# Expert weights split during the first attention, its stack laid out in one piece, and one batch instead of two held for the end

## What is computed

```python
x = x + attn0(layernorm(x))        # 16 heads, weights replaced by their signs times a mean
x = x + cross0(layernorm(x), ctx)
x = x + ffn0(layernorm(x))
x = x + attn1(layernorm(x))        # 4 global and 12 windowed heads
x = x + cross1(layernorm(x), ctx)
x = x + moe(layernorm(x))
...
shared = jax.nn.silu(xt @ sg_w.T) * (xt @ su_w.T) @ sd_w.T
logits = xt @ router_w.T + routing_bias
topk_p, topk_idx = jax.lax.top_k(jax.nn.sigmoid(logits), 2)     # of 8 experts
h = jax.nn.silu(einsum('th,eih->tei', xt, wg)) * einsum('th,eih->tei', xt, wu)
routed = einsum('te,teh->th', w, einsum('tei,ehi->teh', h, wd))  # w: the two normalised probabilities
return shared + routed
```

## Time and profile before

| | |
|---|---|
| median of 3 runs | 2143.51 us (2140.32, 2143.51, 2156.59) |
| the profiled run | 2145.49 us |
| its span | 2143.4 us |
| PE busy | 1688.7 us (79%) |
| DVE busy | 1316.8 us (61%) |
| ACT busy | 1118.9 us (52%) |
| POOL busy | 979.4 us (46%) |
| granted clock of PE, mean | 0.889 |
| DMA | 130.26 MB, mean 61 GB/s |

### The profile page before, as it was taken

The page is one execution under the profiler, slowest core; times in us unless marked ns, Lnnn a source line. Parts: engine busy times, 40 slices in busy tenths (PEclk is TensorE's granted clock), DMA queues, the critical chain, the costliest instruction groups (busy, mean ns, idle before and its releaser), DMA issues. The chain is left out here.

```text
span 2143.4 us, 36053 instructions
## 1 busy us (share of the span) xinstructions
PE 1688.7 (79%) x12334; PEld 859.7 (40%) x12350; DVE 1316.8 (61%) x3599; ACT 1118.9 (52%) x1534; POOL 979.4 (46%) x987
## 2 busy tenths in 40 slices
PE   4888888888688887477777776577747779999997
PEld 2122222222245455123333333344424446666664
DVE  2666777777157897246666664455448865555555
ACT  2366676676445796245555554255446634444442
POOL 3144554541347630456777766255327751212222
PEclk8588999999789999669999988699968889999999
DMA  5331334330040000333333320322224432222216
GB/s 102 65 58 36 62 65 65 61 50 1 5 122 1 1 1 5 52 53 51 54 53 53 58 41 11 84 53 58 47 88 133 132 126 54 61 62 62 58 41 245
DMA packets 114435, 130.26 MB, mean 61 GB/s; under 512 B 22108, under 2 KB 98908, under 8 KB 114108
## 3 DMA queue, kind: packets, MB, share of 16 engines
q1 hardware_dynamic: 107780, 109.74, 25.0%
q0 software_dynamic: 6480, 18.23, 2.2%
HBM read 79.25 MB, written 47.55 MB: 59 GB/s over the span
## 5 line engine op out<-in xcount | busy, mean ns | idle before, releaser
L653 ACT ACTIVATE at_pexp<-ps 128x1024 f32<-128x1024 f32 (+3 forms) x480 | 385.8, 826 | 194.3 <-PE ps L890 193.1
L714 DVE TENSOR_REDUCE at_mx<-ps 128x1 f32<-128x512 f32 x512 | 324.2, 684 | 146.9 <-PE ps L897 144.9
L897 PE MATMUL ps<-at_ks,at_qs 48*128 48x512 f16 (+3 forms) x1024 | 288.7, 357 | 91.6 <-DVE at_mx L714 42.4
L161 PE MATMUL ps<-mo_wall,mo_xt 128*128 x1704 | 301.5, 327 | 1.0 <-DVE mo_xt L2540 0.5
L890 PE MATMUL ps<-at_qs,at_ks 50*128 50x512 f16 (+4 forms) x1024 | 249.7, 341 | 27.7 <-DMA at_qs<-at_mhl 23.1
L950 PE MATMUL ps<-at_pexp,at_vaug 128*32 128x512 f32 (+4 forms) x2048 | 223.4, 529 | 13.9 <-issue 11.2
L161 PEld LDWEIGHTS ps<-mo_wall,mo_xt 128*128 128x128 f16 x1704 | 161.2, 98 | 94.6 <-issue 3.5
L2304 POOL DMA_INDIRECT mo_yd<-mo_xn,mo_idu x71 | 68.1, 959 | 275.8 <-DVE mo_xn L2561 267.0
L716 DVE CUSTOM_DVE_ANT_0 at_junk<-ps,at_lmask 128x192 bf16<-128x192 f32 x384 | 115.5, 353 | 78.7 <-PE ps L897 77.5
L897 PEld LDWEIGHTS ps<-at_ks,at_qs 48*128 48x128 f16 x1024 | 75.6, 98 | 206.1 <-DVE at_mx L714 122.6
L2364 ACT ACTIVATE mo_sg<-ps 128x512 f32<-128x512 f32 x71 | 42.4, 597 | 186.9 <-PE ps L161 186.9
(11 more groups left out here) (396 smaller groups left out, 3853.2 us busy)
## 6 DMA issues: line engine op xcount, KB each, us to landing
at_qs<-at_scratch SPq DMA_DIRECT2D x96, 128.0 KB, 7.2
at_ks<-at_scratch SPq DMA_DIRECT2D x96, 128.0 KB, 7.8
mo_xw<-mo_xs SPq DMA_DIRECT2D x71, 136.0 KB, 2.4
at_scratch<-at_qkh SPq DMA_DIRECT2D x64, 128.0 KB, 1.8
at_scratch<-at_qkl SPq DMA_DIRECT2D x64, 128.0 KB, 1.8
mo_wall<-mo_yd SPq DMA_DIRECT2D x16, 512.0 KB, 10.8
x_qs<-x_queries SPq DMA_DIRECT2D x48, 128.0 KB
mo_stage<-in_m_gate SPq DMA_DIRECT2D x9, 512.0 KB, 3.9
```

The source lines that it names most:

```text
L161: last = nc.tensor.matmul(out, lhs, rhs, start=(n == 0), stop=(n == len(terms) - 1))
L653: last = act.activation(columns(pexp[:, U % 2, hh], at, n, stride, width), columns(banks(r, ST[S % 2], 2), at, n, stride, width), ACT.Exp, ...
L714: last = ve.reduce_max(out, score, AX.X)
L897: return nc.tensor.matmul(banks(r, MX[i % 2])[:, piece.at:piece.at + piece.n], qs[rows, (n // 2) % 2, h // 2, piece.idx * P:(piece.idx + 1 ...
```

## The change

**Weights.** The nine sets of expert weights are split in attention 0 instead of in the experts' stage, on POOL instead of ACT and DVE. `split_lin` becomes 66 chunks: the 12 of before and 54 of the experts (six for each set). They stand at nine slots of a period (`CHUNK_AT`) instead of two; the three POOL operations of a chunk come a slot after its load. The experts' halves go to a tile `whalves`, and four slots after the load SP writes them to a DRAM tensor `moe_weights` (`keep_halves`). The experts' stage reads them from there, the shared expert's set in one DMA and the eight others in one each, the next after two further turned inputs (`xt_ready`). The last chunk stands at slot 229 of 256.

**Stack.** The DRAM buffer of queries and keys is laid out as the stack itself is. A `save` is now three DMAs for a tile (the high half goes twice), a `stack` four DMAs for a batch instead of twelve, each to 48 partitions, in pieces of 8 KB. The same goes for cross-attention 1: six saves instead of two, two stack DMAs instead of six.

**Experts.** Without the SPLIT table ROUTE and SHARED have other places, the shared expert of seven batches (FIRST = 7) runs ahead of the blocks, with the last of these products behind block 0's gate and up, and one batch is held for the end.

```diff
@@ attention_phase
+CHUNK_AT = (1, 3, 5, 14, 15, 17, 28, 29, 31)
+CHUNK_DO = (1, 1, 1, 4)
...
+            whalves = sb("whalves", [P, 2, 2, WCHUNK], F16)
...
-        scratch = nc.dram_tensor(f"{tag}_scratch", (nb, 2, P, 4, T), F16, kind="Internal").ap()
+        scratch = nc.dram_tensor(f"{tag}_scratch", (nb, 2, 2, 3 * DH, NP_, T), F16, kind="Internal").ap()
...
+        MOE_CHUNKS = 6 * (E_ + 1)
+        CHUNKS = LIN_CHUNKS + MOE_CHUNKS
+
+        def chunk_at(i):
+
+            return CHUNK_AT[i % len(CHUNK_AT)] + K * (i // len(CHUNK_AT))
...
             def save(b, m):
-                to = scratch[b] if b < nb else r.x1_queries[b - nb]
+                of_k, par = divmod(m, 2)
+                to = scratch[b, of_k, par] if b < nb else r.x1_queries[b - nb, par]
                 sp.wait_ge(qkh_ready, qk_before(b) + m + 1)
-                sp.dma_start(to[0, :, m, :], qkh[:, m, :]).then_inc(saved, 16)
+                for rep in (0, 1 + of_k):
+                    sp.dma_start(to[rep * DH:(rep + 1) * DH].rearrange("d i t -> i d t"), qkh[:, m, :]).then_inc(saved, 16)
                 sp.wait_ge(qkl_ready, qk_before(b) + m + 1)
-                sp.dma_start(to[1, :, m, :], qkl[:, m, :]).then_inc(saved, 16)
+                rep = 2 - of_k
+                sp.dma_start(to[rep * DH:(rep + 1) * DH].rearrange("d i t -> i d t"), qkl[:, m, :]).then_inc(saved, 16)
 
             def stack(b):
                 p = b % 2
-                sp.wait_ge(saved, 128 * (b + 1))
+                sp.wait_ge(saved, 4 * 48 * (b + 1))
...
                 for par in range(2):
-                    for rep, (qpart, kpart) in enumerate(((0, 0), (0, 1), (1, 0))):
-                        rows = slice(64 * par + 16 * rep, 64 * par + 16 * rep + 16)
-                        sp.dma_start(qs[rows, p], scratch[b, qpart, :, par, :].rearrange("(i d) t -> d i t", d=DH)).then_inc(stacked, 16)
-                        sp.dma_start(ks[rows, p], scratch[b, kpart, :, 2 + par, :].rearrange("(i d) t -> d i t", d=DH)).then_inc(stacked, 16)
+                    rows = slice(64 * par, 64 * par + 3 * DH)
+                    for of_k, to in enumerate((qs, ks)):
+                        sp.dma_start(to[rows, p].rearrange("p i t -> p (i t)"), scratch[b, of_k, par].rearrange("p i t -> p (i t)")).then_inc(stacked, 16)
...
+            def keep_halves(j):
+                s, n, half = moe_chunk(j)
+                sp.wait_ge(lin_done, 2 * (LIN_CHUNKS + j + 1))
+                at = n * NW + half * WCHUNK
+                sp.dma_start(r.moe_weights[s, :, :, at:at + WCHUNK], whalves[:, j % 2]).then_inc(halves_out[j % 2], 16)
...
-                if binary and t >= 0 and t % (K // 2) == 4 and t // (K // 2) < LIN_CHUNKS:
-                    load_lin(t // (K // 2))
+                if binary:
+                    for i in chunks(t):
+                        load_lin(i)
+                    for i in chunks(t - CHUNK_DO[3]):
+                        if i >= LIN_CHUNKS:
+                            keep_halves(i - LIN_CHUNKS)
@@ experts_phase
-SPLIT = {"LOAD": (-105, -83, -71), "WHI": (-58, -42, -34), "WLO": (-42, -28, -19)}
-SPLIT_PERIOD = 35
-FIRST = 6
+FIRST = 7
...
+            sp.dma_start(sh[:].rearrange("p q n w -> p (q n w)"), r.moe_weights[0].rearrange("p q w -> p (q w)")).then_inc(sh_in, 16)
+            for e in range(E):
+                sp.wait_ge(xt_ready, 2 * (e + 1))
+                sp.dma_start(wall[:, e * EW:(e + 1) * EW], r.moe_weights[1 + e].rearrange("p q w -> p (q w)")).then_inc(wall_in, 16)
...
-            early, late = HELD
+            held = HELD[0]
             for i in range(NI):
-                hidden(early, i)
-            add(0)
-            hidden(late, 0)
...
+                hidden(held, i)
+                add(i)
+            for b in range(NI, held + 1):
+                add(b)
+            finish(held)
```

More of the change, by code:

```diff
@@ L289, in attention_phase @@
             wstage = sb("wstage", [P, 2, WCHUNK])
+            whalves = sb("whalves", [P, 2, 2, WCHUNK], F16)
+            halves_out = [sem(f"halves_out{i}") for i in range(2)]
             x_in = [sem(f"x_in{b}") for b in range(nb)]
@@ L354, in attention_phase, with chunks, moe_chunk @@
         LIN_CHUNKS = NC * NLIN // WCHUNK
+        MOE_CHUNKS = 6 * (E_ + 1)
+        CHUNKS = LIN_CHUNKS + MOE_CHUNKS
+        def chunk_at(i):
+            return CHUNK_AT[i % len(CHUNK_AT)] + K * (i // len(CHUNK_AT))
+        def chunks(t):
+            return [i for i in range(CHUNKS) if chunk_at(i) == t]
+        def moe_chunk(j):
+            return j // 6, j % 6 // 2, j % 2
         def main_at(t):
@@ L583, in _ @@
                     normalise((t - place["NORM"]) // K)
-                if binary and t >= K // 2 and t % (K // 2) == 4 and t // (K // 2) - 1 < LIN_CHUNKS:
-                    split_lin(t // (K // 2) - 1)
+                if binary:
+                    for i in chunks(t - CHUNK_DO[0]):
+                        scale_chunk(i)
+                    for i in chunks(t - CHUNK_DO[1]):
+                        chunk_high(i)
+                    for i in chunks(t - CHUNK_DO[2]):
+                        chunk_low(i)
         @block.scalar
@@ L1755, in stack @@
                 if b >= AHEAD:
[L1756 to L1760 removed]
+                    sp.wait_ge(saved, 96 * (b - AHEAD + 1))
+                for par in range(2):
+                    sp.dma_start(qs[64 * par:64 * par + 3 * DH, p].rearrange("p i t -> p (i t)"), r.x1_queries[p, par].rearrange("p i t -> p (i t)")).then_inc(stacked[p], 16)
             def rows(b):
@@ L2128, in experts_phase @@
         sh = sb("sh", [P, 2, 3, NW], F16)
-        stage = sb("stage", [P, 3, NW])
         xw = sb("xw", [P, 3, NJ, 2 * ROW], F16)
@@ L2162, in experts_phase @@
         yb = wall[:, 0:8 * 4 * BT].bitcast(F32).rearrange("p (b k c) -> p b k c", k=2, c=BT)
-        (rw_in, bias_in, w_hi, w_lo, rw_hi, rw_lo, consts, made) = (
-            sem(n) for n in ("rw_in", "bias_in", "w_hi", "w_lo", "rw_hi", "rw_lo", "consts", "made"))
-        w_in = [sem(f"w_in{n}") for n in range(3)]
+        (rw_in, bias_in, sh_in, wall_in, rw_hi, rw_lo, consts, made) = (
+            sem(n) for n in ("rw_in", "bias_in", "sh_in", "wall_in", "rw_hi", "rw_lo", "consts", "made"))
         (hi_ready, lo_ready, turned, xt_ready, lg_done, lg_ready, pr_ready) = (
@@ L2311, in _ @@
         def _(act):
-            def split(s, n):
-                act.wait_ge(w_in[n], 16 * (s + 1))
-                act.activation(part_of(s, 0)[:, n * NW:(n + 1) * NW], stage[:, n, :], ACT.Copy, scale=WS).then_inc(w_hi, 1)
             def high(b):
@@ L2358, in _ @@
                     sigmoid(b)
-                for s, n in due(t, "WHI"):
-                    split(s, n)
             def block_squash(k):
@@ L2400, in settle @@
                 ve.wait_ge(step, steps.n)
-            def split(s, n):
-                ve.wait_ge(w_hi, 3 * s + n + 1)
-                part = slice(n * NW, (n + 1) * NW)
-                ve.scalar_tensor_tensor(out=part_of(s, 1)[:, part], in0=stage[:, n, :], scalar=WS, in1=part_of(s, 0)[:, part],
-                                        op0=ALU.mult, op1=ALU.subtract).then_inc(w_lo, 1)
             def apply(b):
@@ L2534, in _ @@
                         update(b, half).then_inc(x_done, 1)
-                for s, n in due(t, "WLO"):
-                    split(s, n)
             def block_in(k):
@@ L2592, in finish @@
                     update(b, half).then_inc(sum_ready, 1)
-            early, late = HELD
+            held = HELD[0]
             for i in range(NI):
-                hidden(early, i)
-            add(0)
-            hidden(late, 0)
-            add(1)
-            hidden(late, 1)
-            add(2)
-            hidden(late, 2)
-            hidden(late, 3)
-            add(3)
-            add(4)
-            add(5)
-            add(early)
-            finish(early)
-            add(late)
-            finish(late)
+                hidden(held, i)
[3 more added lines that the diff above has]
+            finish(held)
         @block.tensor
```

94 lines of the change are left out of this document (51 added, 43 removed).

## The result

The changed kernel took 2176.61 us in the median of four runs (2172.26 to 2182.38) where the kernel before took 2142.87, a ratio of 1.0152 (95% interval 1.0119 to 1.0185). The forecast was 2132, with a range of 2106 to 2164. It is slower by 34 us, not faster by 11. A second set of runs beside another group of kernels gave 2179.32 us and 1.0175 (1.0139 to 1.021), so the size is firm.

The account below looks back on a forecast made before the run. TensorE, fed by DVE, was to bound attention 0, and chains between engines the experts' front. Terms 19 - 8 - 6.5 - 2.5 - 7 - 6.5 = -11.5 on 2145.5 gave 2134, median 2132 us, range 2106 to 2164.

Parts of the forecast that it names:

- What bounds, and the mechanism: Attention 0: TensorE sets the pace, POOL has 28 us a period spare, but a late `split_max` costs in full.
- The term for POOL's lateness: Attention 0, `split_max` at slot 11: late by 23.3 us in all, +19 us after 4 given back.
- I take that for the chunk as well, since it is queued behind that load: 339.6.: Attention 0, first chunk's load: 4.7 us from issue to landing, as the input's load takes.
- I take 7, nearer to the fast row: Attention 0, stack transfer: 7 us, between 3.8 at 412 GB/s and 13.9 at 113 GB/s.
- for two without I take 2.8.: Attention 0, two periods without an input load: `split_max` 2.8 us late in each.
- I give back 4: Attention 0: PE, idle 8.2 us a period, makes good a little after stalls, 4 us off the lateness of 23.3.
- The rival of the falling clock: Attention 0: the clock falls behind each of six stalls, +10 to +20 us, 2142 to 2152; chance 0.13.
- The rival on the other side: Attention 0 and starts: stack stays at 113 GB/s, +58 instead of +19, 2183 to 2190 us; chance 0.08.
- The starts: First scores wait less for the first stack: -8 us in attention 0, -6.5 in attention 1, -2.5 in cross-attention 1.
- The front: Experts' stage before the blocks: removed splits outweigh the added batch, -7 us, bounds +5 and -20.
- the end: After the blocks: fewer hidden products and one update leave the transfer as floor, -6.5 us.
- It fills gaps: Experts' front: the added batch's 15.9 us on PE fill idle time, leaving 20 of 31.5 us idle.

Follow-up runs that it names:

- the run with two loads ahead: Changed kernel, loads of the two chunks before the first `add_out` issued at slots 19 and 20 instead of 28 and 29: 2159.83 us, ratio 1.009.
- the kernel with stores ahead: Changed kernel with other chunk slots, and the stores of the two chunks before the first `add_out` issued at slot 29, before the stack: 2131.77 us, ratio 0.9934.
- the layout alone: Kernel before the change with only the new stack layout, in both attentions and cross-attention 1: 2135.19 us, ratio 0.9969.
- the kernel with two held batches: Later chunk slots and early stores as above the stack, but the old experts' order, ROUTE and SHARED (six batches ahead), against the changed kernel: 2119.11 us, ratio 0.9884.
- two queues: Kernel with two held batches, but ScalarE issues the upper half (partitions 64 to 111) of each attention's first stack: 2119.47 us, ratio 0.9853.
- The three kernels at 2119 us: The kernel with two held batches (2119.11 us), the same with new ROUTE and SHARED (2118.79), and the same with two queues (2119.47).

## Why the prediction was wrong

**What bounds, and the mechanism: right.** POOL had its time to spare in the mean, `split_max` at slot 11 had none, and six of the `split_max` at slot 11 started behind a chunk instead of behind DVE. That is the place the prediction named, and the chunk took what it said (2.97 us for 2.9).

**The term for POOL's lateness: the step that failed.** It was to be 4.3 us in a period with an input load and 2.8 without. TensorE's six waits were 6.8, 8.9, 10.4, 10.1, 5.1 and 9.9 us, 51.1, of which 3.6 had been there before: 47.5 instead of 23.3 (in the second profile of the changed kernel 44.9, so 41). In the period followed above `split_max` was 9.4 us late. Of the 5.1 more, 1.85 came from the first load, 2.7 from the third and 0.6 from the work itself, 23.2 us for 22.6:

- *"I take that for the chunk as well, since it is queued behind that load: 339.6."* The first chunk was to start 8.3 us after POOL became free; it was 10.15. SP issued the load 4.6 us after and not 3.6, behind saves that had grown by half, and it took 5.5 us to land and not 4.7.
- *"I take 7, nearer to the fast row"*: the third chunk's load, queued behind the stack, was to land 16.4 us after POOL was free, just before POOL came to it. It landed after 21.4, and POOL waited 2.70 us. The stack behind the later first load takes some 10 us and not 7. That the load also had to wait for its buffer, which the prediction left out, made it land 0.4 us later in this period (14.1 us for 13.7 after the stack's first DMA), and 1.4 in the mean of six, by comparison with the run with two loads ahead.
- *"for two without I take 2.8."* Where there is no input load, the first wait is 2.5 us shorter (7.7 and 7.4), but the third chunk waited 3.3 and 4.4. There was no row for these two numbers; they were a guess below the first. For the last period 0.5 was taken for having two chunks fewer; the trace shows all six ahead of it, and TensorE still waited only 0.7 us.

The two waits also stand in for each other: with the first one gone, in the run with two loads ahead, POOL waited 12 us for the load behind the stack.

**"I give back 4": wrong.** Nothing was given back. PE's busy time in the stage is the same in both kernels (364.4 and 364.8 us) and its clock fell from 0.95 to 0.91, so it made up for nothing. The rival of the falling clock held beside the forecast and not instead of it, and smaller than its 10 to 20 us. With 47.5 us of added waits, the remaining 5 of the 52.5 in the table stand beside that drop, which no run separated; against the kernel with stores ahead, at 0.96, PE's busy time is 8 us longer.

**The rival on the other side** had the wrong cause. It said slower from a mean lateness of 5.75 us in seven periods, which counts on starts that gain only 3 us; with the 30.5 us of the forecast's other terms it would have taken 7.4. The mean was 6.8 (47.5 by 7), and the other stretches of the table gave only 15 us together. Its chance of 0.08 rested on the stack at its old speed, while a stack between the two and a later first load led to the same place.

**The starts: right in sign, less than half in size.** On record 17 us for three starts; the layout alone gave 7. In attention 0 the stack went out 1.2 us later than before (33.2 for 32.0), behind the saves, and from there it was to be 9 us and was 12.5 (33.2 to 45.7). In attention 1 TensorE waited 5.19 us for the stack instead of 6.87, so 1.7 less and not 6.5, and in cross-attention 1 12.23 for 13.64. In attention 1 the stack went out 1.8 us after the last save had been issued before the change (879.7 to 881.5) and 3.6 after it (933.2 to 936.8; 2.7 in the kernel with two held batches).

The Trainium skill (DMA: Bandwidth & Descriptors, "Why a DMA increments its semaphore by 16 and not by 1") says that a DMA runs on the largest number of engines up to 16 that divides the slowest dimension of both its sides, 8 for the new saves. This case's trace agrees in direction, 3.6 us for 1.8, but the third save adds bytes as well, and no run parts the two. The prediction set it aside as a fraction of a microsecond. From the Trainium skill (SBUF — State Buffer, "Door 1: The DMA port swizzle") the prediction had worked out an estimated 4.8 us for the stack if its two halves overlap and 9.6 if they don't. The trace agrees with the second: 1.57 MB in the 10 us at 157 GB/s. With two queues it moved 208 GB/s, so that the halves overlap only in part.

**The front and the end: right in sum, wrong in their parts.** The front was to give 7 us and gave 10.1 in this profile (8.6 before the statistics, 1.5 behind them); the end was to give 6.5 and gave 5.8. But *"It fills gaps"*, of the added batch, was false. With six batches ahead the front is 146.6 us, 22 less than before: that is what the removed splits give behind the statistics, 15 of it in PE's idle time and 7 in its busy time at a higher clock. The seventh batch takes 11 to 23 of them back (fronts of 159.4 to 169.3 against 146.6 to 148.3), and gives 5.7 at the end. The prediction reduced PE's idle time from 31.5 to 20 us in its window and let the batch fill gaps; in the changed kernel it is 30.0 (165.0 less 134.97), and it is about the same with and without the batch (28 to 32 us of the front against 29 to 32). The batch's products stand at the end of PE's stream ahead of the blocks, where PE has little idle time to fill, and were priced at 15.9 us beside the 21 measured.

## What to carry to other kernels

Filling an engine's idle time costs nothing only if what the work needs has arrived by then. Follow each added step back through all its waits: the load (what is ahead of it in the issuing engine's stream and in the queue) and the buffer that the result needs (what is ahead of the store that empties it). Here one took the other's place: a load behind the saves and the input, then a load behind the stack, then a store behind the stack. The stage took 465 us in the changed kernel, 414 with the same work ordered ahead of this traffic, and 411 without the work. The buffer that a load needs belongs on the list too, but here it moved the landing by 1.4 us at most in the mean. And when work is removed from the engines that a stage waits for, read where in the stream its gaps are before giving it more. The three kernels at 2119 us (ratios 0.9853 to 0.9884) keep the split in attention 0 with the later slots, and hold two batches back.

## What the runs showed of the hardware

- A 256 KB load issued behind a 512 KB load landed 5.5 us after its issue. Behind a stack of 1.57 MB on the same queue it landed 8.2 us after an issue 5.8 us behind the stack's first, and 11.9 us after one 1.8 us behind it. The quickest of the 66 loads landed in 2.5 us, and their median is 3.0.
- A stack to 48 partitions in 8 KB pieces moved at 157 to 164 GB/s with no other transfer beside it, one to 16 partitions in 1 KB pieces at 113, and two queues for its two halves at 208.
- POOL's operations took the same time (1.04, 0.61 and 1.15 us) before and after: `tensor_tensor` of a chunk took 1.035 to 1.047 us in all 66 of the changed kernel, with DVE busy for 66% of the stage and the DMA queues moving 111 GB/s instead of 51.
